# The two MLP layers of a factorization tower in half-array products over the ring of U blocks

## The reference

```python
p = e[:, ROW_IDX]                                  # (1024, 496, 64)
q = e[:, COL_IDX]
z = jnp.einsum('bne,hne,bnh->bn', p, kernel, q)    # kernel: (64, 496, 64)
h = jnp.concatenate([z, dense_ctx], axis=1)        # (1024, 512)
h = jnp.maximum(h @ W_top1 + b_top1, 0.0)          # 512 -> 512
h = jnp.maximum(h @ W_top2 + b_top2, 0.0)          # 512 -> 256
y = h @ W_top3                                     # 256 -> 1
```

## Time and profile before

| what | us |
|---|---|
| median of 3 runs | 458.8 |
| lowest and highest of them | 458.59, 459.0 |
| the profiled execution | 458.65 |
| its span, first to last instruction | 456.8 |

### The profile page before, as it was taken

The page is one execution under the profiler, slowest core; times in us unless marked ns, Lnnn a source line. Parts: engine busy times, 40 slices in busy tenths (PEclk is TensorE's granted clock), DMA queues, the critical chain, the costliest instruction groups (busy, mean ns, idle before and its releaser), DMA issues.

```text
span 456.8 us, 13200 instructions
## 1 busy us (share of the span) xinstructions
PE 396.6 (87%) x4464; PEld 290.8 (64%) x4464; DVE 358.7 (79%) x513; ACT 319.0 (70%) x2881; POOL 242.4 (53%) x260
## 2 busy tenths in 40 slices
PE   0537678799998999999899998999999998899997
PEld 0324555557776676667666686667676775668775
DVE  0337766479988989888898988888888988899982
ACT  1235647379684987588785888588785978489863
POOL 6655564555655555566555656555656655561000
PEclk9999889799999999999999999999999999999999
DMA  3564660101111111111111111111111110110000
GB/s 75 169 221 165 196 172 18 21 17 22 25 22 23 22 24 21 24 21 24 21 24 25 20 24 21 24 21 23 24 24 22 22 23 20 24 23 13 2 2 1
DMA packets 14563, 19.25 MB, mean 42 GB/s; under 512 B 7192, under 2 KB 7840, under 8 KB 14496
## 3 DMA queue, kind: packets, MB, share of 16 engines
q0 software_dynamic: 8192, 8.40, 9.2%
q1 hardware_dynamic: 6304, 10.00, 6.9%
HBM read 18.39 MB, written 0.00 MB: 40 GB/s over the span
## 4 chain that ended last, share of the span: by engine, by line
PE 78%; DVE 8%; issue 7%; DMA 3%; POOL 2%; another core or an unknown queue 1%; ACT 0%; DVEq 0%
PE u_ps L579 28%; PE u_ps L586 23%; PE side_ps L600 13%; PE side_ps L634 6%; DVE prod_t L489 3%; PE u_ps L564 3%; PE side_ps L645 3%; DMA emb<-tbl,ids_sb 3%; DVE prod_s L507 3%; POOL emb L366 2%; DVE emb_t L476 1%; PE u_ps L665 1%; PE side_ps L658 1%; PE side_ps L626 0%
## 5 line engine op out<-in xcount | busy, mean ns | idle before, releaser
L408 ACT ACTIVATE prod_s<-prod_s 128x64 f32<-128x64 f32 x1405 | 294.4, 336 | 124.6 <-DVE prod_s L507 67.2
L366 POOL DMA_INDIRECT emb<-tbl,ids_sb x256 | 242.2, 946 | 172.2 <-PE u_ps L579 48.0
L408 ACT ACTIVATION_READ_ACCUMULATOR prod_s<-prod_s 128x1 f32 x1405 | 272.9, 250 | 5.5 <-issue 5.4
L489 DVE TENSOR_TENSOR prod_t<-u_ps,emb_t 128x1024 f32<-128x1024 f32 x128 | 156.0, 1219 | 47.7 <-PE u_ps L579 18.7
L579 PEld LDWEIGHTS u_ps<-emb_t,k_sb 64*128 64x128 f32 x2048 | 135.8, 194 | 59.9 <-issue 20.4
L507 DVE TENSOR_TENSOR prod_s<-u_ps,emb 128x512 f32<-128x512 f32 (+4 forms) x224 | 151.6, 721 | 20.5 <-PE u_ps L586 16.7
L579 PE MATMUL u_ps<-emb_t,k_sb 64*128 64x128 f32 x2048 | 149.2, 286 | 19.7 <-DVE emb_t L476 7.0
L586 PE MATMUL u_ps<-k_sb,emb_t 64*128 64x512 f32 (+6 forms) x704 | 133.4, 492 | 12.1 <-DVE prod_t L489 4.9
L586 PEld LDWEIGHTS u_ps<-k_sb,emb_t 64*128 64x128 f32 x704 | 64.6, 195 | 38.3 <-issue 19.4
L600 PE MATMUL side_ps<-prod_t,pick_sb 128*32 128x256 f32 x1024 | 67.7, 384 | 2.2 <-issue 2.0
L520 DVE TENSOR_REDUCE h<-prod_s 128x4 f32<-128x256 f32 x128 | 52.3, 409 | 0.0
(11 more groups left out here) (24 smaller groups left out, 34.4 us busy)
## 6 DMA issues: line engine op xcount, KB each, us to landing
k_sb<-k_pairs SPq DMA_DIRECT2D x9, 512.0 KB, 4.1
emb<-tbl,ids_sb POOLq DMA_INDIRECT x256
k_sb<-k_pairs SPq DMA_DIRECT2D x6, 480.0 KB
w_sb<-w SPq DMA_DIRECT2D x1, 1024.0 KB
w_sb<-w SPq DMA_DIRECT2D x1, 512.0 KB
k_sb<-k_pairs SPq DMA_DIRECT2D x1, 448.0 KB, 3.7
h<-dense SPq DMA_DIRECT2D x8, 8.0 KB
out<-y_row SPq DMA_DIRECT2D x8, 0.5 KB
```

Of the source, the lines that this page charges most:

```text
L366: nc.gpsimd.indirect_dma_start(emb[t % EMBS][:, f * EMBED:(f + 1) * EMBED], None, tables[f], bass.IndirectOffsetOnAxis(ap=ids_sb[:, t, f:f ...
L408: done = nc.scalar.activation(slot, slot, ACT.Copy, accum_out=acc_ps[:, t % 2, column:column + 1])
L489: done = nc.vector.tensor_tensor(prod_t[at % TRING][:].rearrange("p (h x) -> p h x", h=HALVES), u, low.unsqueeze(1).to_broadcast([P, HALVE ...
```

## The change

The three calls of hidden layers become six pieces, and their output moves from `side_ps` into the ring.

- Every product over 128 rows is cut into two over 64 rows. `layer(t, phase)` computes a pair of output blocks (m, m+1). In the first phase of a pair rows 0 to 63 of the array add to block m in the first bank of a slot while rows 64 to 127 add to block m+1 in the second bank; in the second phase (`swapped`) the halves change places. Each phase is 16 matmul records per four c and two halves, that is eight products over 64 rows.
- A pair takes a slot of the ring with its first phase and holds it over the block between the phases, the second phase, and ScalarE's two activations, which read it (`relu`). `PHASES_AT` puts the six phases after blocks 8, 9, 11, 12, 16 and 17.
- ScalarE's ReLUs become three calls of two activations: before its sums of block 7, after six of its twelve sums of block 9, and at block 16 (`RELU_AT`). `sum_block` can be done in two parts for this.
- The slots emptied by ScalarE are counted by a semaphore of their own (`mlp_emptied`), the others as before (`EMPTIED`).
- Tables: `order` has other kinds at blocks 18, 21, 23 and 25 (n = 17 to 20 are now all straight, 21 and 22 turned, 23 straight, 24 to 26 turned); turn(2) follows block 10 and not 12; the logit and the first picks follow block 22 and not 23; a gather that waited for the fourth of four MLP steps waits for the fifth of six phases.

```diff
-    order = "SSSTTSSSTSSTTTST" "TSTSSSTTTSTSTTST"
+    order = "SSSTTSSSTSSTTTST" "TSSSSTTSTTTSTTST"
-TURN_AT = {3: 1, 12: 2}
+TURN_AT = {3: 1, 10: 2}
+PHASES_AT = {8: 0, 9: 1, 11: 2, 12: 3, 16: 4, 17: 5}
+RELU_AT = {0: (7, 0), 1: (9, 6), 2: (16, 0)}
+PAIRS_OF_OUTPUTS = 3
+PHASES = 2 * PAIRS_OF_OUTPUTS
...
+            if t > 0 and n in PHASES_AT and PHASES_AT[n] % 2 == 0:
+                uses.append(("mlp", t - 1, PHASES_AT[n] // 2))
...
-LATE_SPREAD_AT, HIDDEN1_AT, LATE_HIDDEN1_AT, HIDDEN2_AT, SUMS_AT, LATE_SUMS_AT, SPREAD_AT = 3, 8, 12, 18, 23, 27, 31
+LATE_SPREAD_AT, SUMS_AT, LATE_SUMS_AT, SPREAD_AT = 3, 22, 27, 31
...
+            def relu(t, pair):
+                act.wait_ge(mlp_part, PHASES * t + 2 * pair + 2)
+                u = u_ps[SLOT_USE["mlp", t, pair] % USLOTS]
+                for half in range(2):
+                    to, bias, m = (h1_t, b1_sb, 2 * pair + half) if pair < 2 else (h2_t, b2_sb, half)
+                    done = nc.scalar.activation(to[:, m], u[:, half * BANK:half * BANK + P], ACT.Relu, bias=bias[:, m:m + 1])
+                done.then_inc(mlp_emptied, 1)
...
-            def hidden1(t, portion):
-                if portion == 0:
-                    pe.wait_ge(side_copied, STEPS * t + 1)
-                for m in range(2 * portion, 2 * portion + 2):
-                    for c in range(4):
-                        done = nc.tensor.matmul(side_ps[:, m], w1_sb[:, c, m * P:(m + 1) * P], h0_t[:, c],
-                                                start=(c == 0), stop=(c == 3))
...
+            def layer(t, phase):
+
+                pair, swapped = phase // 2, phase % 2 == 1
+                at = SLOT_USE["mlp", t, pair]
+                if swapped:
+                    pe.wait_ge(mlp_part, PHASES * t + phase)
+                    u = u_ps[at % USLOTS]
+                else:
+                    u = slot_free(at)
+                    if pair == 0:
+                        pe.wait_ge(side_copied, t + 1)
+                    if pair == 2:
+                        pe.wait_ge(mlp_emptied, PAIRS_OF_OUTPUTS * t + 2)
+                weights, x, first = (w1_sb, h0_t, 2 * pair) if pair < 2 else (w2_sb, h1_t, 0)
+                for c in range(4):
+                    for half in range(2):
+                        rows = slice(half * P // 2, (half + 1) * P // 2)
+                        of = 1 - half if swapped else half
+                        m = first + of
+                        done = nc.tensor.matmul(u[:, of * BANK:of * BANK + P], weights[rows, c, m * P:(m + 1) * P],
+                                                x[rows, c], start=(not swapped and c == 0), stop=(swapped and c == 3))
+                done.then_inc(mlp_part, 1)
```

88 lines of the change are left out of this document (34 added, 54 removed), and 2 rows, old and new, of the table GATHER_AT.

## The result

The changed kernel is slower. Over four runs of each on one chip it takes 481.27 us (479.48 to 482.09) where the kernel before takes 458.69 (458.23 to 459.0): 1.0488 times as long, 95% interval 1.0455 to 1.0521. The forecast was 456.1 us, with a range up to 461.5. The profiled run took 482.09 us, with a span of 480.3 against 456.8.

The account below looks back on a forecast made before the run. VectorE was taken to bound u(8) to u(22), with held signals eating the ring's cushion. 5 x (-0.45 - 0.25) + 0.6 + 0.25 = -2.65 took the profiled 458.65 to 456.0, forecast 456.1 us, range 449.5 to 461.5.

Parts of the forecast that it names:

- What bounds the kernel: From u(8) to u(22): VectorE is the bound, the ring's three slots the cushion, despite TensorE busy 87% of the span.
- held signals: TensorE's block-full word reaching VectorE late during gathers: 2.5 us per tile before, walked to -0.45 a tile in the new order.
- The walk through the ring: Tile 4 from u(8) in the new order: without late signals 1.1 us idle, a stretch of 20.05, 0.5 us longer.
- the signs that the prediction named for its own failure: Turn(2), `late_sums` or straight blocks waiting for ScalarE, a phase over 0.95 us, or late signals depending on the new order.
- Cost nothing; if that cover is gone, 0.5 us a tile.: ScalarE's activations and sums: 3.1 to 4.6 us idle in the stretch covers sums coming up to 2 us later.
- Turn(2), nothing or 0.2 us: The earlier turn's gathered data arrive just when the slot is free; at most 0.2 us on TensorE, hidden by u(10).
- The picks after 22, -0.25: Logit and first picks after u(22): VectorE's idle time behind the picks shrinks, 0.25 us less a tile.
- TensorE's own time, counted nothing: Half-array phases give back 0.1 to 0.2 us in each of 21 calls, 2 to 4 us in all, none counted directly.
- Tile 1, +0.6: Tile 1 keeps its third turn after block 12, so u(13) waits for the activations behind phase 3: +0.6 us.
- A, the cushion is gone: Rival: late signals go straight to VectorE's idle time while pairs hold slots; 461.4 us, 467 at full price; chance 0.29.
- B: Rival: half pieces fill the waits, so slot waits hide late signals, stretch 20.1, 448.9 us; chance 0.20.
- The 0.57 for a gain: Chance given to the whole kernel being faster by over 0.2%: the forecast's 0.37 and the much-faster rival's 0.20.

Follow-up runs that it names:

- e5: The changed kernel itself, unaltered, in a series without held signals: 405.42 us, 1.0102 times the kernel before.
- e17: Changed kernel with one GpSimd gate moved (the gather that waited for block 9 waits for block 10), with held signals: 471.19 us, ratio 1.0243 to the kernel before.
- e11: Changed kernel with the old tables (block kinds, third turn after 12, picks after 23), with held signals: 489.99 us, ratio 1.0520 to the kernel before.
- e18: Changed kernel with its six pieces as whole-array products into `side_ps`, no ring slot borrowed, with held signals: 468.86 us, ratio 1.0207 to the kernel before.
- e13: The changed kernel itself again, in another series without held signals: 406.06 us, 1.0103 times the kernel before.
- e3: Changed kernel with GpSimd's gathers gated by VectorE's slot release instead of TensorE's signals, without held signals: 437.8 us, ratio 1.0899 to the kernel before.
- e6: The kernel before itself, unaltered, one run for its trace in a series without held signals: 402.49 us.
- e12: Changed kernel with whole-array products, each piece one output block in the same slots, with held signals: 485.28 us, ratio 1.0418 to the kernel before.
- e4: Kernel before with GpSimd's gathers gated by VectorE's slot release instead of TensorE's signals, without held signals: 409.4 us, ratio 1.0192 to the kernel before.

## Why the prediction was wrong

**What bounds the kernel.** Right: VectorE's work stayed the same, and the waits told the story. Also right that held signals are the largest thing in the stretch. Wrong was to take them as a fixed 2.5 us a tile that the new order would redistribute.

**The walk through the ring.** Right, to within 0.1 us at each wait, where no signal is held. It said 0.1, 0.5 and 0.5 us at u(10), u(13) and u(18); e5 has 0.15, 0.43 and 0.54. It gave a stretch of 20.05 us; e5 has 20.37, of which 0.33 is one reduction more that the new order puts ahead of u(22) (VectorE busy 19.25 against 18.91), and which is missing behind it.

**The step that failed: held signals on the new order.** Two of the signs that the prediction named for its own failure came: turn(2) waits for ScalarE, and the held signals depend on what the new order changes. The text said "I let a signal that falls due within about 0.8 us after the end of a gather wait until then, and kept the gathers' pace." Three things in it, or left out of it, were wrong.
- The pace did not keep. The walk read tile 4 of the old order, where the third gather came at 262.45, 1.69 us after the one before it; in tiles 2, 3, 5 and 6 that kernel already had three in a row, 1.25 us apart. GpSimd's own gates are signals of TensorE and of the layers; it went in rows of three over phase 1 and u(10), and the rows' holds joined. Measured in tile 4: 1.43 at u(10) where the walk said 0.6, 1.86 at u(13) where it said 0.8, 0.76 at u(16) where it said nothing, and 0.27 at u(18) where it said 0.95. With one gather less in the row (e17) u(10) has 0.15.
- The walk sent held signals to VectorE alone. The first pair's signal goes to ScalarE, and TensorE needs that slot back: 2.02 to 2.07 us of idle time on TensorE in the middle of the ring (2.17 to 2.27 in e11). In e18, without borrowed slots, TensorE waits 0 to 1.21 us at that place, for the turn's data.
- After such a wait TensorE's clock fell to half in two tiles, 1.6 to 1.8 us each. The prediction had no term for it.

Together the stretch became 25.06 us, not 21.6.

**ScalarE: "Cost nothing; if that cover is gone, 0.5 us a tile."** The cover was reckoned in ScalarE's busy time. It went in another way: ScalarE was idle for 2.14 us because its signal was held. Busy time was no measure of it.

**Turn(2), nothing or 0.2 us.** Under-sized. Without holds TensorE waits 0.17 us for the data in tile 4 of e5, and in e13 0.67 and 0.54 us in tiles 4 and 5. With holds it waits for them 0.68 to 1.89 us in tiles 2 to 6 of e17. e3 shows how little room the earlier turn leaves.

**The picks after 22, -0.25.** Not found. Without holds VectorE waits 0.30 us at u(23) in e5 and 0.33 at u(24) in e6, a gain of 0.03. With holds it is 2.18 in tile 4, where the kernel before has 0.33: a loss of 1.85. e17 and e18 have it too (e18 1.77), so it is not the ring's. It is the largest single wait of VectorE in that tile, and no experiment moved it alone. e11, with the old tables, waits only 0.9 to 1.7 us behind the picks, and is no faster.

**TensorE's own time, counted nothing.** Right as far as the runs show. From start to start a phase takes 0.89 us (272.73 to 273.62), two of them 1.78 where the whole-array call took 1.99, so the estimate of 0.1 to 0.2 us a call held. (The page's 49.0 us for L665 can't be set beside the 44.2 of L634 and L645: the 42 pieces overlap their neighbours more often than the 21 calls did, and two of them ran at half clock.) No run shows that this time bought anything: e12, with whole-array products, has a ratio that is no higher. By the Trainium skill (TensorEngine Tiling, Performance Considerations, PSUM Bottleneck) tiling speeds up TensorE but not the emptying of PSUM, and e12 agrees.

**Tile 1, +0.6.** Under-sized. e5's tile 1 is 1.3 us longer than e6's (48.55 against 47.29), with 1.51 us at u(13) where the steps gave 0.3. With holds it is 2.8.

**The rivals.** A, the cushion is gone, named the side and the place. Its mark of 3.1 us of idle time in the stretch was passed (24.33 less 19.72 is 4.6 in tile 4), though its waits "ahead of most blocks" did not come; its full price of 467 us was still 14 short, for it had neither the way through ScalarE nor the joined holds nor the clock. B is refuted: the waits for slots did not hide held signals. The 0.57 for a gain rested on one walk with holds, whose inputs were read from the old order.

**What stays open.** What puts a chip in the condition with holds isn't known; one chip showed both. Whether the wait of GpSimd or its transfer holds the signals was to be told by e3 and e4, and wasn't, since both fell in a series without holds. The other half of the loss was not taken apart: in e17 VectorE still waits 1.1 to 1.9 us at u(13) and 1.5 to 2.2 at u(23) in tiles 2 to 6. e17 and e18 don't add up to a full account: between e18 and the changed kernel the slots, the form of the products and ScalarE's earlier reads all differ. The changed kernel itself ran with holds in one series only, and e17 and e18 in another.

## What to carry to other kernels

Before a buffer ring lends a slot to work that a third engine must finish, follow the signal of that work, not the engine's busy time: a late signal to the third engine stops the ring, while a late signal to the bound engine may fall into time it has left over. Where a disturbance is tied to events (here gathers), its price in a new order is not its old price: list which event lies over which signal in the new order, and count events in a row as one long one. Tables that set an order belong to one layout of the work; the new ones cost the old kernel 10.9 us without holds, though the prediction took them for harmless.

## What the runs showed of the hardware

- The same kernel on the same chip takes 401 us in one series and 465 in another. What the traces show to differ: in the slow condition signals of TensorE arrive late while gathers are under way. In the trace of before 138 of 255 counts of `slot_filled` are over 0.15 us late, in that of e6 none of 279; VectorE's are late in neither. VectorE's first tile takes 53.6 us from u(0) to u(0) in e6 and 76.0 in the trace of before, and a tile with gathers 45.4 against 51.0; a tile without gathers is nearly the same (the stretch of tile 7 takes 19.53 and 19.54).
- With holds, the signals read above were delivered 1.68 us (ScalarE in e17) and 1.81 us (changed kernel, third gather) after the start of a gather. Of all late counts of `slot_filled`, 103 of 138 in the trace of before lie 1.4 to 2.1 us after some gather's start; the others don't. Without holds the same signal takes 0.03 us (e5).
- The granted clock fell from 1.00 to 0.50 for 3.4 us right after TensorE had been idle for 2.07 us, and for 2.04 us in tile 5 (0.51 in its window): in two of five tiles with such a wait. In e11, with waits of 2.17 to 2.27 us in the same five tiles, it fell in tile 6 alone (0.94 over its stretch); with waits of 0.7 us in three tiles and 1.7 to 1.9 in two, in e17, it never fell there. By the Trainium skill (TensorE: Matmul & The Clock Gate, Part 1: The HAM clock gate) an idle array runs at 1.2 GHz and a busy one at 2.4 GHz; the 0.50 and 1.00 of this trace are these two levels.
